# Eight batches written out in a cross-attention kernel, and a third of the query moves issued by ScalarE

## The chip, the cores and the metric

The kernel runs on one core of one Trainium2 chip. The metric is the device time of one execution in microseconds (us); lower is better. Before the change it is the median of three runs.

## The reference

Eight batches of 256 tokens of 256 features attend to 1601 context rows of 64 features, with 16 heads, and a small feed-forward network follows. Cut to what matters:

```python
q_big = jnp.einsum('bshk,hkq->bshq', (layernorm(x) @ Wq.T).reshape(b, s, H, K), w_kc_q)
kv_rope = kv_c * cos + rotate_half(kv_c) * sin
q_r = jnp.einsum('bshq,hqr->bhsr', q_big, W_qr)
k_r = jnp.einsum('bld,hdr->bhlr', kv_rope, W_kr)
attn = softmax(einsum('bhsr,bhlr->bhsl', q_r, k_r))
ctx_c = jnp.einsum('bhsl,bld->bhsd', attn, kv_rope)
x = x + einsum('bhsd,hkd->bshk', ctx_c, w_kc_kv).reshape(b, s, H * K) @ Wo.T
# ffn: thought = mlp(last token of layernorm(x)), 4 steps; gate = sigmoid(x @ gate_w + gate_b)
x = x + layer_norm(x + gate * (thought @ bc_w + bc_b))
```

## The kernel before

**The prologue** folds the weights, so that a head's query is one product of the normalised x with a 256x64 matrix, and the attended context is projected by one folded matrix. It then makes the queries of the first two head pairs.

**The main part** takes the 8 batches one after the other. A batch `n` has 8 head pairs (`p`, and `g = 8n + p` over all), a pair has 13 slots (`t`, the key tiles of 128 rows, the last of 65). In a slot TensorE (`pe`) does, in this order: the scores of tile `t` into one of two PSUM banks `ps_s` (lines 741 and 742, high and low parts of the queries in `qq[p % 4]`); a tile of scores of the *next* pair, only for its row maxima (`maxima`, line 614, into `ps_m`); and the products of probabilities and keys of the tile six slots back (`p_kv`, lines 660, 663 and 670). ScalarE (`act`) takes the exponential of each score tile (line 469); GpSimd, for two tiles of 13 VectorE, makes the low parts of the probabilities (line 210); VectorE reads the maxima (line 936). The scores of slot `t` may start when the exponential of slot `t - 2` is done, since that one frees the bank.

**The queries of pair g + 2** are made in slot 3 of pair g: six matmuls (line 602) into `ps_x`, a copy to `q_hi` by ScalarE (`high_part`, after the exponential of slot 3), and in slot 4 the rest to `q_lo` by VectorE (`low_part`). Both hold the two heads of a pair in rows 0 to 63 and 64 to 127. `qq` wants each head's 64 rows side by side in columns, the high part in rows 0 to 63 and once more in rows 64 to 127, the low part in rows 0 to 63. That is six DMAs of 64 rows by 512 bytes for a pair, all issued by SyncE (`sp`) in `move_queries` (lines 247 to 258): four for `q_hi` as soon as it is there, two for `q_lo`. They count on `in_qq[p % 2]`. TensorE waits for all six (line 748, in slot 10 of pair g) ahead of the first maxima of pair g + 2; ScalarE and VectorE wait for them much later, before they overwrite `q_hi` and `q_lo`.

**The loop.** Every engine's program goes through `batches` (line 212): batch 0 is written out, batches 1 to 6 are a hardware loop (`Fori`) of three rounds of two batches each, and batch 7 is written out. So a jump back is taken twice, between batches 2 and 3 and between batches 4 and 5. Waits in the loop compare with values computed from the loop's register.

**Other work in a batch**: in pair 4, after `high_part` of slot 3, ScalarE also normalises the rows of the batch before (`normalise_u`, line 510); in pair 6 it does a gate there, in pair 2 a copy in slot 2. SyncE loads the keys of the next batch (lines 237 and 238), and copies turned keys (`move_keys`).

**The end** is the last token's network, a chain of small steps, the gating, a layer norm and the store.

Of the kernel before, what the change touches and what calls it, by code (L numbers as in the profile page):

```python
# [15 lines left out]
B, S, DM = 8, 256, 256  # L16
# [6 lines left out]
NP = H // 2  # L23
# [31 lines left out]
def build_xattn_ffn(nc, x, kv, kv_last, cos_n, sin_n, ident_in, sel_in, wq, wkcq_t, wkckv, wqr, wkr_t, wo_t,  # L55
                    in_gamma, in_beta, agg_w, agg_b, pn_gamma, pn_beta, d1_w, d1_b, d2_w, d2_b,
                    bc_w, bc_b, gate_w, gate_b, out_gamma, out_beta, out):
    with ExitStack() as ctx:
# [150 lines left out]
            r = 128 if t < KT - 1 else LAST  # L209
            eng.tensor_tensor(probs_lo(t)[0:r, :], probs(t)[0:r, :], probs_hi(t)[0:r, :], ALU.subtract).then_inc(done, 1)  # L210

        def batches(eng, batch):

            batch(0, 0)
            with eng.Fori(0, (B - 2) // 2) as i:
                batch(i * 2 + 1, 1)
                batch(i * 2 + 2, 0)
            batch(B - 1, 1)

        def first(n):  # L220
            return isinstance(n, int) and n == 0

        def last(n):
            return isinstance(n, int) and n == B - 1


        @block.sync
        def _(sp):
            sp.dma_start(ident[:, :], ident_in).then_inc(in_small, 16)
            sp.dma_start(wkcq2[0:DCQ - 128], wkcq_t[128:DCQ]).then_inc(in_wa, 16)  # L230
            sp.dma_start(wqr2[0:DCQ - 128], wqr[128:DCQ]).then_inc(in_wa, 16)
            xv = xs[:, :].rearrange("p (b s m) -> p b s m", b=B, s=ST)
            for b in range(0, B, 2):
                sp.dma_start(xv[:, b:b + 2], x[b:b + 2].rearrange("b (s p) m -> p b s m", p=128)).then_inc(in_x[b // 2], 16)

            def load_keys(n):
                sp.dma_start(raw[:, 0:KT - 1, :], kv[n]).then_inc(in_raw, 16)
                sp.dma_start(raw[0:LAST, KT - 1, :], kv_last[n]).then_inc(in_raw, 16)

            sp.dma_start(sinn[:, :, :].rearrange("p t d -> p (t d)"), sin_n).then_inc(in_tab, 16)  # L240
            sp.dma_start(cosn[:, :, :].rearrange("p t d -> p (t d)"), cos_n).then_inc(in_tab, 16)
            sp.wait_ge(pads, 1)
            load_keys(0)
            sp.dma_start(wos, wo_t).then_inc(in_wc, 16)
            sp.dma_start(wkckvs, wkckv).then_inc(in_wc, 16)

            def move_queries(p, g):

                sp.wait_ge(qh_done, g + 1)
                if not (isinstance(g, int) and g < 4):  # L250
                    sp.wait_ge(st_done, g * KT - 3 * KT)
                d, r = qq[p % 4], p % 2
                for h in range(2):
                    for j in range(2):
                        sp.dma_start(d[64 * j:64 * j + 64, 0, h * S:(h + 1) * S], q_hi[r][64 * h:64 * h + 64, :]).then_inc(in_qq[r], 16)  # L255
                sp.wait_ge(ql_done, g + 1)
                for h in range(2):
                    sp.dma_start(d[0:64, 1, h * S:(h + 1) * S], q_lo[r][64 * h:64 * h + 64, :]).then_inc(in_qq[r], 16)

            def move_keys(n, par, i):  # L260

                sp.wait_ge(kt_copied, n * 2 + (i + 1))
                sp.dma_start(k_hx[par][0:64, key_half(i)], k_hl[par][0:64, key_half(i)]).then_inc(in_kx, 16)

            move_queries(0, 0)
            move_queries(1, 1)
            for i in range(2):
                move_keys(0, 0, i)
            sp.dma_start(gw[:, :, :], gate_w.rearrange("(t p) m -> p t m", p=128)).then_inc(in_gate, 16)
            sp.dma_start(gb[:, :], gate_b.partition_broadcast(128)).then_inc(in_gate, 16)  # L270
            for dst, src in ((aggs, agg_w), (bcs, bc_w)):
                sp.dma_start(dst[:, :, :], src.rearrange("(t p) m -> p t m", p=128)).then_inc(in_ffn, 16)
            for dst, src in ((ogs, out_gamma), (obs, out_beta)):
                sp.dma_start(dst[:, :], src.partition_broadcast(128)).then_inc(in_ffn, 16)
            for dst, src in ((ig8, in_gamma), (ib8, in_beta), (pg8, pn_gamma), (pb8, pn_beta), (ab8, agg_b), (db8, d2_b), (bb8, bc_b)):
                sp.dma_start(dst[:, :], src.partition_broadcast(B)).then_inc(in_ffn, 16)
            sp.dma_start(d1bs[:, :], d1_b).then_inc(in_ffn, 16)
            sp.dma_start(sels[:, :, :], sel_in).then_inc(in_ffn, 16)

            def batch(n, par):  # L280
                sp.wait_ge(prep, (n + 1) * PREP_OPS)
                if not last(n):
                    load_keys(n + 1)
                else:
                    for i, (src, w) in enumerate(((d1_w, HID), (d2_w, DM))):
                        sp.dma_start(tables[:, i * 2 * HID:(i + 1) * 2 * HID].rearrange("p (t m) -> p t m", m=w),
                                     src.rearrange("(t p) m -> p t m", p=128)).then_inc(in_dw, 16)
                for p in range(NP - 2 if last(n) else NP):
                    move_queries((p + 2) % NP, n * NP + p + 2)
                    if not last(n) and p in (3, 5):  # L290
                        move_keys(n + 1, 1 - par, (p - 3) // 2)

            batches(sp, batch)
            sp.wait_ge(x_saved, B)
            sp.dma_start(th[:, :], xs[127:128, :].rearrange("p (b s m) -> p b s m", b=B, s=ST)[:, :, ST - 1, :]).then_inc(in_row, 16)
            for b in range(B):
                sp.wait_ge(final[b % 2], b // 2 + 1)
                sp.dma_start(out[b].rearrange("(s p) m -> p s m", p=128),
                             gates[:, b * XB:(b + 1) * XB].rearrange("p (s m) -> p s m", s=ST)).then_inc(stored, 16)
            sp.wait_ge(stored, 16 * B)  # L300
# [3 lines left out]
        def _(pool):  # L304
# [45 lines left out]
                        if not first(n) and (p, t) in ROOT_SLOTS:  # L350
                            newton(n - 1, ROOT_SLOTS[p, t])

            batches(pool, batch)

            pool.wait_ge(pv_done, B * TB)
            for i in range(3):
# [25 lines left out]
        def _(act):  # L382
# [51 lines left out]
            def high_part(p, g):  # L434

                act.wait_ge(q_done, g + 1)
                copy(q_hi[p % 2][:, :], ps_x[:, 0:S], scale=SC / SW).then_inc(qh_done, 1)

            def copy_row(p, g):

                act.wait_ge(mrow_done, g + 1)
                copy(qq[p % 4][64:65, 1, :], ps_x[64:65, :], scale=1.0 / SC).then_inc(mrow_copied, 1)
# [4 lines left out]

            act.wait_ge(pads, 15)
            high_part(0, 0)
            high_part(1, 1)  # L450
            for i in range(2):
                copy_keys(0, 0, i, first_key_bank(i))
            for i in range(4):
# [5 lines left out]
            def batch(n, par):  # L459
                for p in range(NP):  # L460
                    g = n * NP + p
                    started = not (first(n) and p == 0)
                    for t in range(KT):
# [8 lines left out]
                        if t == 3 and not (last(n) and p >= NP - 2):  # L472
                            act.wait_ge(in_qq[p % 2], n * (QQ_DMAS * 4) + QQ_DMAS * (p // 2 + 1))
                            high_part(p, g + 2)
                        if t == 8 and started:
                            ctx_high(par if p else 1 - par, (p - 1) % NP, g - 1)
                        if t == 11 and not (last(n) and p == NP - 1):
# [21 lines left out]

            def save_x(m):  # L500
                act.wait_ge(post, m * POST_OPS + 1)
                copy(xs[:, bass.ds(m * XB, XB)], u[:, :, :].rearrange("p s m -> p (s m)")).then_inc(x_saved, 1)

            def normalise_u(m):
                act.wait_ge(root, m * ROOT_OPS + ROOT_OPS)
                for all_, one in ((rs_all, rs), (nm_all, nmu)):
                    copy(all_[:, bass.ds(m * ST, ST)], one[:, :]).then_inc(kept, 1)
                act.wait_ge(x_saved, m + 1)
                for st in range(ST):
                    act.activation(u[:, st, :], u[:, st, :], ACT.Identity, bias=nmu[:, st:st + 1],  # L510
# [2 lines left out]
            def gate(m):  # L513

                act.wait_ge(post, m * POST_OPS + 9)
                act.activation(gates[:, bass.ds(m * XB, XB)], z[:, :, :].rearrange("p s m -> p (s m)"),
                               ACT.Tanh, scale=0.5).then_inc(gate_out, 1)

            batches(act, batch)
            ctx_high(1, NP - 1, B * NP - 1)  # L520
            save_x(B - 1)
            for k in range(2 + K_STEPS):
# [23 lines left out]
        def _(pe):  # L546
# [52 lines left out]
            def queries(n, p, g):  # L599

                for i, (mt, wi, xi) in enumerate(SPLIT_MT):
                    mm = pe.matmul(ps_x[:, 0:S], mw[wi][:, mt, p * 128:(p + 1) * 128], xn_hl[xi][:, bass.ds(n * S + mt * B * S, S)],  # L602
                                   start=(i == 0), stop=(i == len(SPLIT_MT) - 1))
                mm.then_inc(q_done, 1)

            def maxima(par, p, g, j):

                if not (isinstance(g, int) and g == 0 and j < 3):

                    pe.wait_ge(mx_read, g * MX_OPS + {0: -3, 1: 0, 2: -1, MX_OPS - 1: MX_OPS - 2}.get(j, j - 2))  # L610
                if j < MX_OPS - 1:
# [179 lines left out]
                        else:  # L791
                            p_kv(n, par, p, t - LAG)

            batches(pe, batch)
            g = B * NP - 1
            for t in range(KT - LAG, KT):
                p_kv(B - 1, 1, NP - 1, t)
# [57 lines left out]
        def _(dve):  # L855
# [82 lines left out]
            def negate_max(p, g):  # L938

                dve.wait_ge(mx_read, g * MX_OPS + MX_OPS)  # L940
                if not (isinstance(g, int) and g == 0):
                    dve.wait_ge(mrow_done, g)
                with nc.allow_low_precision("a shift that cancels in the softmax"):
                    dve.tensor_reduce(negm[:, :], mxs[p % 2][:, :].rearrange("p (k i) -> p i k", k=4), AX.X, ALU.max,
# [6 lines left out]
            def normalise(p, g):  # L951
# [1 line left out]
                d = sums(p % 2)  # L953
                dve.wait_ge(pv_done, g * KT + KT)
                dve.reciprocal(inv[:, :, :], d[:, :, :, ONE]).then_inc(inv_done, 1)
                if not (isinstance(g, int) and g == 0):
                    dve.wait_ge(ct_done, g)
                dve.wait_ge(inv_done, g + 1)
                dve.tensor_tensor(ctx_m[:, :, :, :].rearrange("p s h d -> p h s d"), d[:, :, :, HIGH:OW],
# [7 lines left out]
            def post_a(m, psum):  # L967

                o = m * POST_OPS
                c = bass.ds(m * XB, XB)  # L970
                dve.wait_ge(proj_done, m * ST + ST)
                dve.wait_ge(st_done, m * TB + TB)
                dve.scalar_tensor_tensor(u[:, :, :], psum, 1.0 / SW, xs[:, c].rearrange("p (s m) -> p s m", s=ST), ALU.mult,
# [70 lines left out]
                            if p == 6 and t == 0:  # L1044
                                post_c(n - 1, ps_x[:, :])

            batches(dve, batch)
            g = B * NP - 1
            normalise(NP - 1, g)
            ctx_low(1, NP - 1, g)  # L1050
# [177 lines left out]
```

## Time and profile before

| | |
|---|---|
| median of 3 runs | 1167.55 us (1167.28 to 1168.71) |
| profiled execution, its own time | 1167.4 us |
| its span, first to last instruction | 1165.6 us |
| TensorE busy | 1073.1 us, 92% of the span |
| GpSimd, VectorE, ScalarE busy | 890.4, 886.5, 657.9 us |
| mean granted TensorE clock | 0.957 of 2.4 GHz |

The span and the time differ by 1.8 us around the program. The rows below come from one profiled execution. Busy shares tell which engine is full on the average; which wait sets the end is read from the waits and from the order in time. A transfer's issue is an instruction of the queue that issues it (SPq for SyncE, ACTq for ScalarE); its landing comes later.

### The profile page before, as it was taken

How to read it: one execution, taken by the hardware profiler on the slowest of the kernel's cores; microseconds unless marked ns; L12 is line 12 of the kernel's file. 1: busy time of each engine (PE TensorE's matmuls, PEld its weight loads, DVE VectorE, ACT ScalarE, POOL GpSimd, SP SyncE). 2: the span in 40 equal slices, each digit the busy share in tenths (PEclk: the TensorE clock that was granted, in tenths of full speed). 3: DMA queues.
4: the chain of work that ended last, by engine and by line, in shares of the span. 5: the costliest groups of instructions: out<-in, count | busy, mean ns of one | idle time of the engine just before them, and what ended most of it. 6: DMA issues, size and time to landing. Idle time of an engine off the chain costs nothing.

```text
span 1165.6 us, 39347 instructions
## 1 busy us (share of the span) xinstructions
PE 1073.1 (92%) x14644; PEld 714.8 (61%) x14644; DVE 886.5 (76%) x1573; ACT 657.9 (56%) x1179; POOL 890.4 (76%) x956
## 2 busy tenths in 40 slices
PE   5799999999999997999999989999999999999361
PEld 4446666666666665666666655666666667667240
DVE  5488888788868885788868776778878786887448
ACT  1546666566656664566656654566656665666322
POOL 0349988798889975898879876898879886878713
PEclk9989999999999998999999998999999999999655
DMA  9120001000100010000100010000100020000002
GB/s 340 48 78 15 21 18 30 16 21 15 30 12 21 18 31 12 14 21 19 30 11 21 17 33 16 9 21 19 30 16 21 15 89 11 15 16 2 1 2 72
DMA packets 42567, 36.37 MB, mean 31 GB/s; under 512 B 7864, under 2 KB 39416, under 8 KB 41920
## 3 DMA queue, kind: packets, MB, share of 16 engines
q1 hardware_dynamic: 41792, 29.49, 8.6%
q10 hardware_dynamic: 576, 4.19, 1.0%
q8 instruction: 129, 2.11, 0.8%
q14 instruction: 70, 0.57, 0.2%
HBM read 17.27 MB, written 2.10 MB: 17 GB/s over the span
## 4 chain that ended last, share of the span: by engine, by line
PE 81%; DVE 8%; issue 4%; DMA 4%; SPq 2%; ACT 1%; POOL 1%; DVEq 0%; ACTq 0%; POOLq 0%
PE ps_s L742 14%; PE ps_s L741 14%; PE ps_m L614 13%; PE ps_o L660 8%; PE ps_o L663 8%; PE ps_o L670 8%; PE ps_x L602 3%; PE ps_x L686 3%; DMA qq<-q_lo 2%; DVE mx L936 2%; PE ps_x L625 2%; SPq L255 1%; PE ps_x L678 1%; PE ps_x L713 1%; DMA plo_all<-wqr_dram 1%
## 5 line engine op out<-in xcount | busy, mean ns | idle before, releaser
L210 POOL TENSOR_TENSOR plo_all<-big 128x512 f16<-128x512 f32 x640 | 689.5, 1096 | 187.7 <-ACT big L469 186.7
L936 DVE TENSOR_REDUCE mx<-ps_m 128x1 f32<-128x512 f32 (+1 forms) x832 | 544.0, 666 | 199.8 <-PE ps_m L614 167.5
L469 ACT ACTIVATE big<-ps_s 128x512 f32<-128x512 f32 x768 | 458.0, 597 | 357.8 <-PE ps_s L742 356.8
L741 PE MATMUL ps_s<-qq,k_hl 128*128 128x512 f16 (+1 forms) x832 | 317.3, 381 | 12.6 <-issue 12.6
L742 PE MATMUL ps_s<-qq,k_hx 96*128 96x512 f16 (+1 forms) x832 | 319.0, 383 | 0.0
L614 PE MATMUL ps_m<-k_hl,qq 128*128 128x512 f16 x768 | 293.8, 383 | 6.7 <-DMA qq<-q_lo 5.5
L660 PEld LDWEIGHTS ps_o<-k,big 128*128 128x128 bf16 x3072 | 186.4, 98 | 122.4 <-issue 2.8
L663 PE MATMUL ps_o<-k,big 128*128 128x64 f16 x3072 | 220.0, 193 | 0.0
L670 PE MATMUL ps_o<-k,plo_all 128*128 128x65 f16 x3072 | 218.8, 193 | 0.0
L660 PE MATMUL ps_o<-k,big 128*128 128x65 f16 x3072 | 218.1, 193 | 0.0
L210 DVE TENSOR_TENSOR plo_all<-big 128x512 f16<-128x512 f32 x128 | 172.4, 1347 | 0.0
L663 PEld LDWEIGHTS ps_o<-k,big 128*128 128x128 bf16 x3072 | 146.6, 98 | 0.0
L670 PEld LDWEIGHTS ps_o<-k,plo_all 128*128 128x128 f16 x3072 | 145.0, 97 | 0.1
L614 PEld LDWEIGHTS ps_m<-k_hl,qq 128*128 128x128 f16 x768 | 76.4, 100 | 107.6 <-DVE mx L936 13.9
L741 PEld LDWEIGHTS ps_s<-qq,k_hl 128*128 128x128 f16 (+1 forms) x832 | 81.7, 98 | 14.4 <-issue 13.8
L742 PEld LDWEIGHTS ps_s<-qq,k_hx 96*128 96x128 f16 (+1 forms) x832 | 82.6, 99 | 1.0 <-issue 0.8
L323 POOL TENSOR_TENSOR tables<-tables 128x256 f32<-128x256 f32 (+3 forms) x64 | 55.1, 861 | 27.1 <-DMA tables<-kv_last_dram 26.5
L210 POOL TENSOR_TENSOR plo_last<-pr_last 65x512 f16<-65x512 f32 x64 | 66.4, 1037 | 1.4 <-ACT pr_last L469 1.3
L602 PE MATMUL ps_x<-xnt,mw 128*128 (+1 forms) x384 | 52.3, 272 | 2.4 <-DVE mw L915 1.4
L602 PEld LDWEIGHTS ps_x<-xnt,mw 128*128 128x128 f16 x384 | 37.1, 97 | 20.9 <-DVE mw L915 1.6
L469 ACT ACTIVATE pr_last<-ps_s 65x512 f32<-65x512 f32 x64 | 38.0, 593 | 14.0 <-PE ps_s L742 14.0
L390 ACT ACTIVATE qq<-ps_x 1x512 f16<-1x512 f32 x64 | 37.6, 588 | 5.7 <-PE ps_x L625 4.1
(189 smaller groups left out, 914.8 us busy)
## 6 DMA issues: line engine op xcount, KB each, us to landing
qq<-q_hi SPq DMA_DIRECT2D x256, 32.0 KB, 1.9
qq<-q_lo SPq DMA_DIRECT2D x128, 32.0 KB, 1.9
tables<-kv_dram SPq DMA_DIRECT2D x8, 384.0 KB
big<-wq_dram ACTq DMA_DIRECT2D x1, 2048.0 KB, 14.9
xs<-x_dram SPq DMA_DIRECT2D x4, 512.0 KB, 17.5
big<-wo_t_dram SPq DMA_DIRECT2D x1, 2048.0 KB, 12.9
tables<-d_w_dram SPq DMA_DIRECT2D x2, 1024.0 KB, 6.8
out_dram<-big SPq DMA_DIRECT2D x8, 256.0 KB, 2.2
```

The source lines that it names most:

```text
L210: eng.tensor_tensor(probs_lo(t)[0:r, :], probs(t)[0:r, :], probs_hi(t)[0:r, :], ALU.subtract).then_inc(done, 1)
L323: pool.tensor_tensor(*ops[k % 6]).then_inc(prep, 1)
L390: return act.activation(out_, in_, ACT.Copy, **kw)
L469: act.activation(probs(t)[0:r, :], ps_s[0:r, (p * KT + t) % 2, :], ACT.Exp, scale=1.0 / SC).then_inc(p_done, 1)
L602: mm = pe.matmul(ps_x[:, 0:S], mw[wi][:, mt, p * 128:(p + 1) * 128], xn_hl[xi][:, bass.ds(n * S + mt * B * S, S)], start=(i == 0), stop=(i ...
L614: mm = pe.matmul(ps_m[:, j % 3, :], qq[p % 4][:, 0, a:a + 128], k_hl[par][:, c:c + 512], start=True, stop=True)
L660: pe.matmul(d[:, q // 2, q % 2, :], probs_hi(t)[:, q * 128:(q + 1) * 128], k3[par][:, t, 0:OW], start=(t == 0 and q == 0), stop=False, ski ...
L663: pe.matmul(d[:, q // 2, q % 2, HIGH:OW], probs_hi(t)[:, q * 128:(q + 1) * 128], k3[par][:, t, LOW:LOW + DC], start=False, stop=False, ski ...
L670: mm = pe.matmul(d[:, q // 2, q % 2, :], probs_lo(t)[:, q * 128:(q + 1) * 128], k3[par][:, t, 0:OW], start=False, stop=(t == KT - 1), skip ...
L741: pe.matmul(ps_s[0:r, j % 2, :], k_hl[par][:, c], qq[p % 4][:, 0, :], start=True, stop=False)
L742: pe.matmul(ps_s[0:r, j % 2, :], k_hx[par][:, c], qq[p % 4][0:96, 1, :], start=False, stop=True).then_inc(st_done, 1)
L936: dve.tensor_reduce(o, i, AX.X, ALU.max).then_inc(mx_read, 1)
```

## The change

The loop is gone: `batches` calls each engine's program for `n` from 0 to 7, all waits and addresses are constants. The second of the two copies of the queries' high half (the one into rows 64 to 127 of `qq`) is issued by ScalarE: after `high_part` in the prologue, and in the main part in slot 4, after the exponential of that slot. SyncE issues the other four.

```diff
-        def batches(eng, batch):
-            batch(0, 0)
-            with eng.Fori(0, (B - 2) // 2) as i:
-                batch(i * 2 + 1, 1)
-                batch(i * 2 + 2, 0)
-            batch(B - 1, 1)
+        def batches(batch):
+            for n in range(B):
+                batch(n, n % 2)
...
                 for h in range(2):
-                    for j in range(2):
-                        sp.dma_start(d[64 * j:64 * j + 64, 0, h * S:(h + 1) * S], q_hi[r][64 * h:64 * h + 64, :]).then_inc(in_qq[r], 16)
+                    sp.dma_start(d[0:64, 0, h * S:(h + 1) * S], q_hi[r][64 * h:64 * h + 64, :]).then_inc(in_qq[r], 16)
                 sp.wait_ge(ql_done, g + 1)
...
+            def move_high(p, g):
+                act.wait_ge(qh_done, g + 1)
+                for h in range(2):
+                    act.dma_start(qq[p % 4][64:128, 0, h * S:(h + 1) * S], q_hi[p % 2][64 * h:64 * h + 64, :]).then_inc(in_qq[p % 2], 16)
...
             high_part(0, 0)
+            move_high(0, 0)
             high_part(1, 1)
+            move_high(1, 1)
...
                         if t == 3 and not (last(n) and p >= NP - 2):
                             act.wait_ge(in_qq[p % 2], n * (QQ_DMAS * 4) + QQ_DMAS * (p // 2 + 1))
                             high_part(p, g + 2)
+                        if t == 4 and not (last(n) and p >= NP - 2):
+                            move_high((p + 2) % NP, g + 2)
```

The rest of the diff replaces `isinstance` tests and `bass.ds` slices by plain ones, since every `n` is now a number.

## Rows read from the trace of the kernel before

**Rows 1.** The page, part 1: busy us, share of the span, instructions of each engine.
```profile
PE 1073.1 (92%) x14644; PEld 714.8 (61%) x14644; DVE 886.5 (76%) x1573; ACT 657.9 (56%) x1179; POOL 890.4 (76%) x956
```

**Rows 2.** TensorE's waits from 60 to 1060 us: total us, times, longest.
```profile
PE ps_s L741 <- issue: 12.6, 2, 6.7
...
PE ps_m L614 <- DMA qq<-q_lo: 1.6, 4, 0.6
```

**Rows 3.** Windows, one batch long each: us, busy us of each engine, then clock.
```profile
216.44:340.81 124.37, 123.95 (x1755) 83.16 (x1754) 100.06 (x171) 76.29 (x138) 107.30 (x115) 1.00 0.08 20
340.81:474.02 133.21, 126.27 (x1755) 84.27 (x1754) 99.43 (x171) 76.29 (x138) 106.94 (x115) 0.97 0.07 20
474.02:598.68 124.66, 124.03 (x1755) 83.15 (x1754) 100.05 (x171) 76.29 (x138) 107.39 (x115) 1.00 0.08 20
598.68:733.01 134.33, 126.67 (x1755) 84.34 (x1754) 99.33 (x170) 76.28 (x138) 106.62 (x115) 0.97 0.07 19
733.01:857.59 124.58, 124.03 (x1756) 83.16 (x1754) 100.14 (x171) 76.30 (x138) 107.42 (x115) 1.00 0.08 20
857.59:981.88 124.29, 123.90 (x1755) 83.12 (x1754) 99.22 (x170) 76.20 (x138) 104.59 (x112) 1.00 0.12 34
```

**Rows 4.** Timeline, first matmuls of batches 3 and 5: start, us; in brackets idle before.
```profile
442.57 0.61 PE L741 MATMUL ps_s<-qq,k_hl 128*128 128x512 f16 x1 [5.93 <-issue]
...
701.19 0.60 PE L741 MATMUL ps_s<-qq,k_hl 128*128 128x512 f16 x1 [6.67 <-issue]
```

**Rows 5.** Windows, right after the first of those: clock behind the busy times.
```profile
442.50:447.10 4.60, 4.53 (x32) 2.49 (x33) 1.38 (x2) 1.20 (x2) 1.80 (x2) 0.52 0.01 4
```

**Rows 6.** Timeline and line view: query moves by SyncE, durations in ns min/median/max.
```profile
514.33 2.38 SPq L255 DMA_DIRECT2D qq<-q_hi  x4
516.75 1.24 SPq L258 DMA_DIRECT2D qq<-q_lo  x2
...
L255 SPq DMA_DIRECT2D qq<-q_hi x256: 461/597/1767, 52.5 to 1038.3; - x128
```

**Rows 7.** Timeline, program start: issues of both queues.
```profile
0.75 0.41 SPq L229 DMA_DIRECT2D ident<-ident_in_dram  x1
0.75 0.41 ACTq L384 DMA_DIRECT2D big<-wkcq_t_dram  x1
...
1.85 0.91 SPq L231 DMA_DIRECT2D plo_all<-wqr_dram  x1
```

**Rows 8.** Timeline, ScalarE in slots 3 to 5 of pair 4, then slot 4 of pair 5.
```profile
514.31 1.08 ACT L510 ACTIVATE u<-u,nmu,rs 128x256 f32<-128x256 f32 x2
515.29 1.06 ACT L469 ACTIVATE big<-ps_s 128x512 f32<-128x512 f32 x2
...
529.47 0.60 ACT L469 ACTIVATE big<-ps_s 128x512 f32<-128x512 f32 x1 [0.41 <-PE ps_s L742]
```

**Rows 9.** Timeline, TensorE: scores of slots 4 and 7 of pair 4, slot 4 of pair 5.
```profile
514.00 0.38 PE L741 MATMUL ps_s<-qq,k_hl 128*128 128x512 f16 x1
...
517.05 0.38 PE L741 MATMUL ps_s<-qq,k_hl 128*128 128x512 f16 x1
...
528.84 0.38 PE L741 MATMUL ps_s<-qq,k_hl 128*128 128x512 f16 x1
```

**Rows 10.** Timeline, the prologue's query moves and what follows.
```profile
52.54 2.43 SPq L255 DMA_DIRECT2D qq<-q_hi  x4
...
53.90 0.38 ACT L390 ACTIVATE q_hi<-ps_x 128x256 f16<-128x256 f32 x1 [1.38 <-PE ps_x L602]
54.18 1.02 ACT L390 ACTIVATE k_hl<-ps_o 128x1024 f16<-128x1024 f16 x1
...
55.01 1.23 SPq L258 DMA_DIRECT2D qq<-q_lo  x2
55.08 0.71 ACT L390 ACTIVATE k_hl<-ps_m 128x640 f16<-128x640 f16 x1
...
57.77 0.59 PE L614 MATMUL ps_m<-k_hl,qq 128*128 128x512 f16 x1 [3.91 <-DMA qq<-q_lo]
```

More of the change, by code:

```diff
@@ L210, in make_low @@
             eng.tensor_tensor(probs_lo(t)[0:r, :], probs(t)[0:r, :], probs_hi(t)[0:r, :], ALU.subtract).then_inc(done, 1)
-        def batches(eng, batch):
-            batch(0, 0)
-            with eng.Fori(0, (B - 2) // 2) as i:
-                batch(i * 2 + 1, 1)
-                batch(i * 2 + 2, 0)
-            batch(B - 1, 1)
+        def batches(batch):
+            for n in range(B):
+                batch(n, n % 2)
         def first(n):
-            return isinstance(n, int) and n == 0
+            return n == 0
         def last(n):
-            return isinstance(n, int) and n == B - 1
+            return n == B - 1
         @block.sync
@@ L249, in move_queries @@
                 sp.wait_ge(qh_done, g + 1)
-                if not (isinstance(g, int) and g < 4):
+                if not (g < 4):
                     sp.wait_ge(st_done, g * KT - 3 * KT)
@@ L291, in batch @@
                         move_keys(n + 1, 1 - par, (p - 3) // 2)
-            batches(sp, batch)
+            batches(batch)
             sp.wait_ge(x_saved, B)
@@ L351, in batch @@
                             newton(n - 1, ROOT_SLOTS[p, t])
-            batches(pool, batch)
+            batches(batch)
             pool.wait_ge(pv_done, B * TB)
@@ L501, in save_x @@
                 act.wait_ge(post, m * POST_OPS + 1)
-                copy(xs[:, bass.ds(m * XB, XB)], u[:, :, :].rearrange("p s m -> p (s m)")).then_inc(x_saved, 1)
+                copy(xs[:, slice(m * XB, (m + 1) * XB)], u[:, :, :].rearrange("p s m -> p (s m)")).then_inc(x_saved, 1)
             def normalise_u(m):
@@ L506, in normalise_u @@
                 for all_, one in ((rs_all, rs), (nm_all, nmu)):
-                    copy(all_[:, bass.ds(m * ST, ST)], one[:, :]).then_inc(kept, 1)
+                    copy(all_[:, slice(m * ST, (m + 1) * ST)], one[:, :]).then_inc(kept, 1)
                 act.wait_ge(x_saved, m + 1)
@@ L515, in gate @@
                 act.wait_ge(post, m * POST_OPS + 9)
-                act.activation(gates[:, bass.ds(m * XB, XB)], z[:, :, :].rearrange("p s m -> p (s m)"),
+                act.activation(gates[:, slice(m * XB, (m + 1) * XB)], z[:, :, :].rearrange("p s m -> p (s m)"),
                                ACT.Tanh, scale=0.5).then_inc(gate_out, 1)
-            batches(act, batch)
+            batches(batch)
             ctx_high(1, NP - 1, B * NP - 1)
@@ L601, in queries @@
                 for i, (mt, wi, xi) in enumerate(SPLIT_MT):
-                    mm = pe.matmul(ps_x[:, 0:S], mw[wi][:, mt, p * 128:(p + 1) * 128], xn_hl[xi][:, bass.ds(n * S + mt * B * S, S)],
+                    mm = pe.matmul(ps_x[:, 0:S], mw[wi][:, mt, p * 128:(p + 1) * 128], xn_hl[xi][:, slice(n * S + mt * B * S, n * S + mt * B * S + S)],
                                    start=(i == 0), stop=(i == len(SPLIT_MT) - 1))
@@ L606, in maxima @@
             def maxima(par, p, g, j):
-                if not (isinstance(g, int) and g == 0 and j < 3):
+                if not (g == 0 and j < 3):
                     pe.wait_ge(mx_read, g * MX_OPS + {0: -3, 1: 0, 2: -1, MX_OPS - 1: MX_OPS - 2}.get(j, j - 2))
@@ L792, in batch @@
                             p_kv(n, par, p, t - LAG)
-            batches(pe, batch)
+            batches(batch)
             g = B * NP - 1
@@ L940, in negate_max @@
                 dve.wait_ge(mx_read, g * MX_OPS + MX_OPS)
-                if not (isinstance(g, int) and g == 0):
+                if not (g == 0):
                     dve.wait_ge(mrow_done, g)
@@ L955, in normalise @@
                 dve.reciprocal(inv[:, :, :], d[:, :, :, ONE]).then_inc(inv_done, 1)
-                if not (isinstance(g, int) and g == 0):
+                if not (g == 0):
                     dve.wait_ge(ct_done, g)
@@ L969, in post_a @@
                 o = m * POST_OPS
-                c = bass.ds(m * XB, XB)
+                c = slice(m * XB, (m + 1) * XB)
                 dve.wait_ge(proj_done, m * ST + ST)
@@ L1045, in batch @@
                                 post_c(n - 1, ps_x[:, :])
-            batches(dve, batch)
+            batches(batch)
             g = B * NP - 1
```

## The prediction

> **What bounds the kernel now.** I read the busy line of the page first: TensorE is busy for 92% of the span, the next engines for 76% [rows 1]. An average can hide a chain through other engines, so the second view is TensorE's waits in the main part. They are short, and two entries matter: 12.6 us in two pieces that wait for nothing the profile shows, and 1.6 us in four pieces for query moves [rows 2]. So over a thousand microseconds TensorE sets the pace, and ScalarE, VectorE and GpSimd count only where they make it wait. The third view cuts the main part into windows that start at the same matmul of each batch. Four of the six last 124.29 to 124.66 us, two last 133.21 and 134.33, with a lower clock in those two and nearly the same work [rows 3]. The timeline shows where: TensorE stands still for 5.93 and 6.67 us ahead of the first matmul of batches 3 and 5 [rows 4]. Those are the two places where a jump back to the loop's head is taken; at the boundaries 1 to 2, 3 to 4, 5 to 6 and 6 to 7, which the four short windows cross, there is no such gap. The last of these is the way out of the loop, so leaving it costs nothing that can be seen.
>
> **The loop written out.** The cost of a jump back is read as a whole from the windows, since it is more than the gap. After the gap TensorE runs at a granted clock of 0.52, that is at 1.2 GHz in place of 2.4, for some 4.6 us, after having been idle [rows 4, 5]. The mean of the four windows without a jump is (124.37 + 124.66 + 124.58 + 124.29) / 4 = 124.48 us. The two with one have 133.21 + 134.33 - 2 x 124.48 = 18.6 us more. Of that 12.6 is the gap, the other 6.0 is the slow clock and two waits for queries that come just behind it. With no jump I take off all 18.6. The low bound of this gain is 12.6, if the clock fell for some other reason; I see no room for more, since the other batches run without gaps. Batch 7 is already written out and takes the same time as a batch in the loop [rows 3]. That prices two things at nothing: constants instead of register values in the waits, and longer straight programs.
>
> **Two issues fewer on SyncE.** The four issues of the high part take 2.38 us, the two of the low part 1.24 [rows 6]; with two of the four gone the last one starts up to 1.2 us sooner. In the main part TensorE waits 1.6 us in all for these moves [rows 2]. Two of the four waits, 0.6 us each, stand in the two long windows and are in the 18.6 already. That leaves 0.4 us; the low part must still be made by VectorE first, so I take 0.2, with 0 and 0.4 as ends. SyncE itself is waiting nearly all the time, and nothing else queues behind these moves that TensorE is waiting for.
>
> In the prologue TensorE waits 3.91 us for the first pair's moves, until 57.77 [rows 10]. Now SyncE issues two high moves from 52.54 to 53.64 and two low ones to about 54.9, where it was 56.2; by that alone TensorE could start 1.3 us sooner. But ScalarE gets four issues in its path. The first two, from 52.5 to 53.6, end before its copy at 53.90. The next two come behind that copy, from about 54.3 to 55.4, and push the two key copies, which ran from 54.18 to 55.79, to 55.4 to 57.0. TensorE waits for both key copies too, so it starts at about 57.15. Gain 0.6, ends 0 and 1.3. The key copies are late next; they are what then ends the wait.
>
> **Two issues more on ScalarE in slot 4.** This is the unknown, 62 times. No row shows ScalarE issuing in the main part. The nearest are SyncE's moves of the same shape: 461 ns for the first of a group, 597 for one behind another [rows 6], so 0.46 + 0.04 + 0.60 = 1.10 us for two. What is queued behind them is the exponential of slot 5, and the scores of slot 7 wait for that one's bank; the low parts that GpSimd makes from it are needed six slots later and have time.
>
> In a usual pair the exponential of slot 4 starts at 529.47, 0.63 us behind its scores at 528.84; the scores of slot 7 start 3.05 us behind those of slot 4 (514.00 and 517.05) [rows 8, 9], so 2.42 us behind the exponential. Two ways to count. If the issues begin when the exponential has been handed over, the next exponential starts about 1.15 us behind it and not 1.02, ends at 1.75, and TensorE has 0.67 us left: cost nothing. If they begin only when it has ended, the next one starts at 0.60 + 0.04 + 1.10 + 0.04 = 1.78 and ends at 2.38. That leaves 0.04 us, from which the hand-over and a weight load, some 0.15 us, are to be paid: a stall of about 0.1 us.
>
> Pair 4 has less cover, because two normalisations of 1.08 us stand between, and the exponential of slot 4 starts at 515.29 [rows 8]. In the first way the next one ends at 515.29 + 1.15 + 0.10 + 0.60 = 517.14, while TensorE wants it at 517.05 [rows 9]: a stall of 0.2 us with the hand-over. In the second it ends at 517.67: 0.75 us. This happens in seven batches.
>
> So the cost is 7 x 0.2 = 1.4 us in the first way, and 55 x 0.1 + 7 x 0.75 = 10.8 in the second. The low end is 0, if the issues can start ahead of the exponential. I take 1.4: in the trace ScalarE's next activation starts before the one before has ended (two in 1.06 us, at 0.60 each [rows 8]), so its queue runs ahead of the engine. A few issues are longer, up to 1767 ns [rows 6]; ScalarE has a third of the issues, and what one of these costs beyond the 0.67 us of cover is some 0.5 us. That is for the range.
>
> **The sum**: 1167.4 - 18.6 - 0.2 - 0.6 + 1.4 = 1149.4 us against the profiled execution's own time (span 1165.6 and 1.8 around it). The median of the runs is 0.15 above that one, so 1149.6.
>
> **Rivals.** *The issues take ScalarE's own time* (the second way): 1149.6 - 1.4 + 10.8 = 1159.0 us. For it: nothing rules out that the queue waits for the engine. Against it: the overlapping activations.
>
> *The two queues exclude each other at issue*, the one that ends slower. Place: slot 4, where SyncE's first high move starts at about 529.17, 0.30 ahead of the exponential. Taken in turns, SyncE from -0.30 to 0.16, ScalarE to 0.8, SyncE to 1.4, ScalarE to 2.05, the exponential of slot 5 ends at 2.75, against 2.42 wanted: with the hand-over a stall of 0.48 us. Times 55, and 0.35 for the seven pairs 4, where SyncE is nearly done first: 29 us, so 1149.6 - 1.4 + 29 = 1177 us. It decides from 0.3 us for each pair on, where it eats the 18 us. Against it: at the program's start both queues have an issue from 0.75 to 1.16, 0.41 us each, side by side; for a little of it: SyncE's third took 0.91 [rows 7].
>
> The Trainium skill, page Perfetto Trace Analysis, section DMA Instruction — HWDGE (DVE, Sync), says that the block that generates descriptors is shared by two sequencers and locked for exclusive use while it is used; that is this rival, and only part of an issue's time would be under the lock. The trace agrees at most in the 0.91 us.
>
> *The gap is not the jump's*, and stays: 1167.6 - 0.8 + 1.4 = 1168 us. Against it: four boundaries of the same code have no gap. *The longer program stalls elsewhere*, by half of what is won: 1158 us; against it, batches 0 and 7 are straight code without such gaps.
>
> **How the numbers follow.** The forecast with its ends (issues between 0 and 4 us) has 0.74, and 1146.5 to 1152.5 us. The issues in ScalarE's own time: 0.14, near 1159. Exclusion of the queues: 0.05 for its full price, and 0.02 for one that just cancels the gain. A gap that stays: 0.01. Stalls elsewhere: 0.04. The range of 8 in 10 is 1146.5 to 1158. 0.2% of this time is 2.3 us, about what can be told from no change; faster by more gets 0.92, within it 0.03, slower 0.05.
>
> **What would show it.** Right: no window of a batch above 125 us; no wait "issue" of microseconds on TensorE; clock near 1.00 from 75 to 1060 us; in slot 4 the exponential of slot 5 starting about 1.15 us behind that of slot 4. Wrong: waits of TensorE's line 741 for ScalarE, some 60 of them; ScalarE's issues at 1 us each; windows of 126 us or more with no gap in them. In the prologue the wait for `qq` should turn into one for `k_hl`, until about 57.15.

## The result and the profile after

The changed kernel takes 1148.38 us (median of 4 runs, 1147.16 to 1152.49), the kernel before beside it 1167.41 us (4 runs). The ratio is 0.9847 with a 95% interval of 0.9816 to 0.9877: 1.5% faster, against a forecast of 1149.6 us. The profiled execution took 1147.16 us with a span of 1145.4. On another chip the same kernel (e8 below) took 1150.49 us, with a ratio of 0.9863 (0.9847 to 0.988): a gain of 16.0 us there and of 19.0 us here. The profiled execution is the fastest of all eight.

The page of the kernel after, part 1, as in [rows 1]:

```profile
PE 1067.0 (93%) x14644; PEld 713.7 (62%) x14644; DVE 883.4 (77%) x1573; ACT 656.4 (57%) x1179; POOL 889.1 (78%) x956
```

TensorE's waits from 60 to 1045 us, which answer to [rows 2]:

```profile
PE ps_x L684 <- DVE ctx_m L965: 1.4, 6, 0.2
PE ps_s L747 <- ACT big L473: 1.4, 3, 0.6
```

The 12.6 us that waited for nothing are gone, and so are the waits for query moves. A small new one stands in their place: three waits for ScalarE's exponential, 1.4 us.

The windows of one batch each, from the same matmul as in [rows 3]:

```profile
215.75:339.91 124.16, 123.93 (x1756) 83.31 (x1754) 98.90 (x170) 76.08 (x138) 107.00 (x115) 1.00 0.08 20
339.91:464.09 124.18, 123.89 (x1755) 83.28 (x1754) 99.82 (x170) 76.09 (x138) 106.45 (x114) 1.00 0.08 20
464.09:588.89 124.80, 124.02 (x1755) 83.28 (x1754) 99.41 (x170) 76.08 (x138) 107.47 (x116) 1.00 0.08 20
588.89:713.05 124.16, 123.55 (x1756) 83.64 (x1754) 100.07 (x170) 75.77 (x138) 106.75 (x115) 1.00 0.08 20
...
sum 745.77, PE 743.25 PEld 500.06 DVE 596.82 ACT 456.34 POOL 639.34; mean PE 123.87 PEld 83.34 DVE 99.47 ACT 76.06 POOL 106.56
```

The second and fourth windows, which held the jumps and took 133.21 and 134.33 us, now take 124.18 and 124.16 at a clock of 1.00. All six sum to 745.77 us, where those of [rows 3] sum to 765.44. That is 19.7 of the 20.2 us between the two profiled executions.

ScalarE in a usual pair (timeline, exponentials of slots 4 and 5) and in pair 4, where the two normalisations stand in the way [rows 8]:

```profile
489.85 0.60 ACT L473 ACTIVATE big<-ps_s 128x512 f32<-128x512 f32 x1 [0.35 <-PE ps_s L748]
489.86 1.12 ACTq L439 DMA_DIRECT2D qq<-q_hi  x2
491.08 0.60 ACT L473 ACTIVATE big<-ps_s 128x512 f32<-128x512 f32 x1 [0.63 <-PE ps_s L748]
...
504.71 0.47 ACTq L439 DMA_DIRECT2D qq<-q_hi  x1
504.92 0.59 ACT L516 ACTIVATE u<-u,nmu,rs 128x256 f32<-128x256 f32 x1
505.21 0.61 ACTq L439 DMA_DIRECT2D qq<-q_hi  x1
505.42 1.11 ACT L473 ACTIVATE big<-ps_s 128x512 f32<-128x512 f32 x2
```

The two issues start 0.01 us after the exponential of slot 4 has started, and the next exponential comes 1.23 us behind it. In pair 4 they start before that exponential does, while a normalisation runs. In the usual pair SyncE's two high moves run beside ScalarE's, 0.33 us ahead of them, and neither pair of issues is drawn out:

```profile
489.53 1.10 SPq L251 DMA_DIRECT2D qq<-q_hi  x2
```

The prologue, as in [rows 10]:

```profile
52.34 1.15 SPq L251 DMA_DIRECT2D qq<-q_hi  x2
52.34 1.41 ACTq L439 DMA_DIRECT2D qq<-q_hi  x2
...
54.22 1.13 ACTq L439 DMA_DIRECT2D qq<-q_hi  x2
54.80 1.47 SPq L251 DMA_DIRECT2D qq<-q_hi  x2
...
55.39 1.02 ACT L386 ACTIVATE k_hl<-ps_o 128x1024 f16<-128x1024 f16 x1 [1.21 <-issue]
56.31 0.70 ACT L386 ACTIVATE k_hl<-ps_m 128x640 f16<-128x640 f16 x1
...
57.11 0.39 PE L620 MATMUL ps_m<-k_hl,qq 128*128 128x512 f16 x1 [3.45 <-ACT k_hl L386]
```

The wait is for the key copies now, as forecast, and ends at 57.11 us, where 57.77 stood. Of these 0.66 us, 0.20 are not the change's: the first query matmuls already start at 51.00 us in this execution and at 51.20 in the one before, so the change gives 0.46.

Here the two queues do get in each other's way, a little. Single issues behind another take 0.60 us on SyncE in the kernel before, and 0.62 in ScalarE's pair from 54.22. But ScalarE's second issue, which starts at 52.91, 0.02 us behind SyncE's second one, takes 0.84 us, and SyncE's from 54.80, 0.07 us behind one of ScalarE's, takes 0.83. That makes the 1.41 and the 1.47 above. No code is fetched in this stretch, and the 1.41 or 1.42 us stand in the same place in e2, e6, e8, e9, e10 and e12.

### The profile page after: what moved, and what is told of

Same layout as the page of the kernel before. It is cut to its first block, busy times and chain, and to the rows that moved or that the text cites. A ratio compares the mean times of both kernels' runs of the same rounds, so it can differ in the third digit from the quotient of the medians.

```text
span 1145.4 us, 35018 instructions
## 1 busy us (share of the span) xinstructions
PE 1067.0 (93%) x14644; PEld 713.7 (62%) x14644; DVE 883.4 (77%) x1573; ACT 656.4 (57%) x1179; POOL 889.1 (78%) x956
## 4 chain that ended last, share of the span: by engine, by line
PE 86%; DVE 8%; issue 2%; ACT 2%; DMA 1%; POOL 1%; ACTq 1%; SPq 0%; DVEq 0%; POOLq 0%
PE ps_s L748 15%; PE ps_s L747 15%; PE ps_m L620 14%; PE ps_o L666 9%; PE ps_o L669 8%; PE ps_o L676 8%; PE ps_x L608 3%; PE ps_x L692 3%; DVE mx L942 2%; PE ps_x L631 2%; PE ps_x L684 1%; PE ps_x L719 1%; DMA plo_all<-wqr_dram 1%; PE ps_s L564 1%; PE ps_s L565 1%
## 5 line engine op out<-in xcount | busy, mean ns | idle before, releaser
L210 DVE TENSOR_TENSOR plo_all<-big 128x512 f16<-128x512 f32 x128 | 168.1, 1314 | 0.0
L608 PE MATMUL ps_x<-xnt,mw 128*128 128x256 f16 x384 | 52.2, 272 | 2.4 <-DVE mw L921 1.4
```

## The experiments

Each is compared with the kernel before on its own chip; its median there was 1167.69, 1166.48 and 1167.17 us for the three sets (e1 to e4, e5 to e8, e9 to e12).

### e1, e2: each half of the change alone

e1 takes the kernel before and writes the loop out on all engines; the moves stay with SyncE. e2 keeps the loop and has only the issues moved.

```diff
# e1
-            batch(0, 0)
-            with eng.Fori(0, (B - 2) // 2) as i:
...
-            batch(B - 1, 1)
+            for n in range(B):
+                batch(n, n % 2)
...
# e2
...
+                        if t == 4 and not (last(n) and p >= NP - 2):
+                            move_high((p + 2) % NP, g + 2)
```

> All engines written out, all six moves issued by SyncE as before. Theory (the jumps are the cost, the issues are hidden): nearly the whole gain, 18 to 19 us, so 1148.5 to 1149.5 us; the wait for queries in the prologue stays, TensorE starts the first maxima at about 57.7 us. Rival (the issues on ScalarE give a good part of the gain): 1155 us or more.

> The loop as before, ScalarE issues the two second copies. Theory: 0.7 us less from the prologue and about as much lost or won in the main part, so within 1.5 us of the kernel before, 1166 to 1168 us, with two gaps of 5.9 and 6.7 us. Rival (the issues give a good part of the gain): 1160 us or less.

e1: 1150.56 us (1149.95 to 1150.63), ratio 0.9848 (0.9831 to 0.9864), 17.1 us less than the kernel before. The loop written out gives the whole gain, within what can be told: the changed kernel gained 19.0 us on one chip and 16.0 on another. Its six windows span 745.77 us (963.63 - 217.86), the same as those of the changed kernel.

e2: 1175.92 us (1168.03 to 1178.49, six runs), ratio 1.0068 (1.0047 to 1.0088). This is a miss of my theory: I expected no change within 1.5 us. The issues alone make the loop kernel 8 us slower in the median, and their cost differs much from run to run. With e9 and e10, which are the same kernel, the median of eight runs is 1173.98 us. The profile is that of the fastest run, and has 8 waits for ScalarE, 3.1 us. e9 and e10 go on from here.

### e3, e4: whose jump it is

In e3 TensorE's program alone is written out, in e4 all others are.

```diff
-        def batches(eng, batch):
+        def batches(eng, batch, flat=False):
+            if flat:
+                for n in range(B):
+                    batch(n, n % 2)
+                return
...
# e3: only this call, e4: the four others
-            batches(pe, batch)
+            batches(pe, batch, True)
```

> TensorE's program alone is written out, the other four engines keep their loop; moves as before. Theory (the gap is TensorE's own, at its jump; what the others lose is hidden by their slack or comes out as a small wait): at most 1151 us, gap gone. Rival (another engine's jump costs as much and only hides beside TensorE's): the gap stays as a wait for ScalarE, VectorE or GpSimd, 1160 us or more.

> Only TensorE keeps the loop, the other four engines are written out; moves as before. Theory: as the kernel before, 1166 to 1168.5 us, with both gaps. Rival (other engines' jumps count): some part of the 18.6 us is gone, 1160 us or less.

e3: 1151.46 us (1150.81 to 1151.78), ratio 0.9855 (0.9838 to 0.9871). e4: 1166.03 us (10 runs), ratio 0.9985 (0.9975 to 0.9995). So TensorE's own jumps carry nearly everything: writing out its program alone gives 16.2 us, writing out the four others alone 1.7. The two windows with the jump in e3, then in e4; the one between them, without a jump, takes 124.16 us in e3 and 124.23 in e4:

```profile
342.02:467.46 125.44, 124.06 (x1756) 83.32 (x1754) 99.22 (x171) 76.02 (x138) 107.24 (x115) 1.00 0.08 20
591.62:716.84 125.22, 124.12 (x1756) 83.26 (x1754) 99.50 (x171) 76.12 (x138) 107.24 (x115) 1.00 0.08 20
```

```profile
342.16:475.09 132.93, 126.39 (x1755) 84.25 (x1754) 99.55 (x171) 76.15 (x138) 106.83 (x115) 0.97 0.07 19
599.32:731.20 131.88, 125.89 (x1755) 84.09 (x1754) 99.98 (x171) 76.15 (x138) 107.14 (x115) 0.97 0.08 19
```

With TensorE running straight, a jump of the others shows as 1.1 to 1.3 us in a window. It is a wait for ScalarE, here around the first of them, in e3:

```profile
PE ps_s L745 <- ACT big L473: 1.0, 1, 1.0
```

What TensorE does in the gap can be seen in part in the DMA view, which lists packets that carry instructions (queue, packets, MB, share). First the gap of the kernel before, 436.4 to 442.6 us, then that of e4, 437 to 444:

```profile
q14 instruction: 7, 0.06, 3.5%
q8 instruction: 2, 0.03, 2.5%
```

```profile
q8 instruction: 2, 0.03, 2.1%
```

In e4, where only TensorE jumps, queue 14 is silent and queue 8 still brings two packets; in e3, where the others jump, queue 14 brings its seven (436 to 442 us). So queue 8 carries TensorE's code, and two blocks of it are fetched while TensorE stands still. The two fetches do not fill the gap of 5.9 us; what the rest of it is stays open.

### e7: one jump in place of two

The loop has two rounds; batches 5 to 7 are written out behind it.

```diff
-            with eng.Fori(0, (B - 2) // 2) as i:
+            with eng.Fori(0, 2) as i:
                 batch(i * 2 + 1, 1)
                 batch(i * 2 + 2, 0)
-            batch(B - 1, 1)
+            for n in range(5, B):
+                batch(n, n % 2)
```

> The kernel before with a loop of two rounds (batches 1 to 4) and batches 5 to 7 written out: one jump back, between batches 2 and 3. Theory (each jump costs 9 us, the loop's code nothing): 9 to 10 us less than before, about 1157.5 us, one gap. Rival (the second gap comes from the place in time, not from the jump): both gaps stay, no change.

1157.68 us (1156.66 to 1159.03), 8.8 us less than the kernel before beside it, where 9 to 10 were expected; ratio 0.9928 (0.9911 to 0.9945). The window between batches 2 and 3 still takes 133.17 us, the one between 4 and 5 takes 124.28:

```profile
341.40:474.57 133.17, 125.93 (x1755) 84.03 (x1754) 100.16 (x171) 76.28 (x138) 106.99 (x115) 0.97 0.07 20
598.94:723.22 124.28, 123.92 (x1755) 83.13 (x1754) 99.99 (x171) 76.38 (x138) 107.31 (x115) 1.00 0.08 20
```

The gap follows the jump, not the place in time; a loop that is entered, and left behind its last round, costs nothing that can be seen.

### e5, e11: what the issues would cost with no cover left

e5 is the changed kernel with all four high moves issued by ScalarE in slot 4.

```diff
-                for h in range(2):
-                    sp.dma_start(d[0:64, 0, h * S:(h + 1) * S], ...)
+                if g < 2:
+                    for h in range(2):
+                        sp.dma_start(d[0:64, 0, h * S:(h + 1) * S], ...)
...
                 for h in range(2):
-                    act.dma_start(qq[p % 4][64:128, 0, h * S:(h + 1) * S], ...)
+                    for j in range(2 if g >= 2 else 1):
+                        r0 = 64 - 64 * j
+                        act.dma_start(qq[p % 4][r0:r0 + 64, 0, h * S:(h + 1) * S], ...)
```

> The changed kernel, but in the main part ScalarE issues all four high moves of a pair (some 2.4 us in place of 1.1), SyncE the two low ones. Theory (the issues start beside the exponential of slot 4, 0.67 us of cover are left): the exponential of slot 5 ends about 3.1 us behind the start of that of slot 4, wanted at 2.42, a stall of 0.7 to 0.8 us in each of 62 pairs: 1190 to 1200 us, with TensorE's line of the high scores waiting for ScalarE. Rival (ScalarE's queue runs further ahead, or an issue does not hold up the next activation): under 1160 us.

1230.32 us (1226.1 to 1234.01), ratio 1.0545 (1.0512 to 1.0578). The direction and the place were right, the size was not. ScalarE's timeline in a usual pair, and TensorE's waits from 75 to 1110 us:

```profile
504.85 0.60 ACT L476 ACTIVATE big<-ps_s 128x512 f32<-128x512 f32 x1 [0.35 <-PE ps_s L751]
504.86 2.41 ACTq L442 DMA_DIRECT2D qq<-q_hi  x4
507.37 1.09 ACT L476 ACTIVATE big<-ps_s 128x512 f32<-128x512 f32 x2 [1.92 <-PE ps_s L751]
```

```profile
PE ps_s L750 <- ACT big L476: 45.4, 61, 2.1
PE ps_m L623 <- DVE mx L945: 21.6, 6, 4.5
```

The first wait is the expected one, 45.4 / 61 = 0.74 us a pair: an issue does hold up the next activation, but not the one that runs. The second wait was expected by nobody. Its longest piece, on VectorE and GpSimd (timeline):

```profile
543.44 7.90 DVE L210 TENSOR_TENSOR plo_all<-big 128x512 f16<-128x512 f32 x1
551.26 1.87 DVE L945 TENSOR_REDUCE mx<-ps_m 128x1 f32<-128x512 f32 x3
```

```profile
544.21 0.86 POOL L320 TENSOR_TENSOR tables<-tables 128x320 f32<-128x320 f32 x1
545.03 2.05 POOL L210 TENSOR_TENSOR plo_all<-big 128x512 f16<-128x512 f32 x2
547.02 1.05 POOL L210 TENSOR_TENSOR plo_last<-pr_last 65x512 f16<-65x512 f32 x1
548.02 0.78 POOL L320 TENSOR_TENSOR k<-tables,k 128x320 f16<-128x320 f32 x1
548.74 2.05 POOL L210 TENSOR_TENSOR plo_all<-big 128x512 f16<-128x512 f32 x2
```

VectorE's low-part instruction (median 1.43 us) takes 7.90 us, to 551.34, while GpSimd has one instruction right behind the other until the last one shown ends at 550.79. A run of GpSimd without a pause is not enough by itself: in the profile of the changed kernel seven low parts of GpSimd follow one another from 146.45 us, and VectorE's, started at 147.88, is through in 2.15 us. e11 tests whether less work on GpSimd ends the long ones: the same kernel, with the low part of one more slot moved from GpSimd to VectorE.

```diff
-LO_D = (2, 9)
+LO_D = (2, 7, 9)
```

> The variant in which ScalarE issues all four high moves (1230 us), with one more low part of the probabilities (slot 7) moved from GpSimd to VectorE. If VectorE's low-part instructions of 8 us are waits for a GpSimd that works without a pause, giving GpSimd an eighth less to do there gives it pauses: these instructions fall to 3 us or less, the waits for the maxima go, and the time falls by 15 us or more, to 1215 us or less. Rival (they have another cause, or VectorE is full): 1225 us or more.

1198.16 us (1197.64 to 1200.2), ratio 1.0272 (1.0255 to 1.0289): 32 us less than e5, although VectorE has 64 instructions more. The low-part instructions of VectorE, min/median/max in ns, and TensorE's waits:

```profile
L210 DVE TENSOR_TENSOR plo_all<-big x192: 677/1353/2736, 78.2 to 1105.7; 128x512 f16<-128x512 f32 x192
```

```profile
PE ps_s L750 <- ACT big L476: 45.0, 62, 1.7
```

The wait for the exponential stays, 45.0 us in 62 pieces, and the waits for the maxima are gone. That bears out that the long instructions come from the work on GpSimd. Whether it is the pauses or the other order of the work that helps was not told apart.

### e6, e12: the prologue

e6 is the changed kernel with the key copies ahead of `move_high(1, 1)`. e12 has ScalarE issue only in the prologue; in the main part SyncE issues all six.

```diff
# e6
             high_part(1, 1)
-            move_high(1, 1)
             for i in range(2):
                 copy_keys(0, 0, i, first_key_bank(i))
+            move_high(1, 1)
# e12
-                        if t == 4 and not (last(n) and p >= NP - 2):
-                            move_high((p + 2) % NP, g + 2)
...
+                    for j in range(1 if g < 2 else 2):
+                        sp.dma_start(d[64 * j:64 * j + 64, 0, h * S:(h + 1) * S], ...)
```

> The changed kernel, but in the prologue ScalarE copies the keys ahead of the second pair's two issues. Theory (the key copies end TensorE's wait at 57.1 us): they end 1.1 us sooner and the wait goes back to the query moves, first maxima at about 56.4 us, 0.5 to 0.8 us less than the changed kernel, about 1147.7 us. Rival (something else ends that wait, or the time is given back before slot 0): no change.

> All engines written out, ScalarE issues only in the prologue, SyncE issues all six moves in the main part. Theory: the prologue's 0.5 us is kept and ScalarE's late activations are gone: 1149.5 to 1150.5 us, the same as the changed kernel within what can be measured, with no wait of TensorE for ScalarE in the main part.

e6: 1148.93 us (1146.42 to 1150.03), ratio 0.9845 (0.9829 to 0.9862); e8 beside it, the changed kernel once more, 1150.49. The wait turned back into one for the moves, 2.8 us where it had been 3.4, which is the 0.6 us expected. (The first maxima come at 57.86 us and not at the expected 56.4, since the query matmuls start at 52.35 us in this execution, 1.35 us later than in the profile of the changed kernel.) Whether the end comes sooner by as much can't be told at this spread.

e12: 1149.3 us (1148.57 to 1150.59), ratio 0.9845 (0.9829 to 0.9862), with no wait of TensorE for ScalarE in the main part. It is as fast as the changed kernel within what can be told. Its four runs lie within 2.0 us, those of the changed kernel within 5.3 and, in e8, within 2.9; four runs are too few to call that a difference in spread.

### e8: the changed kernel again

> The changed kernel once more, beside the other variants of this call: 1148.4 us, the reference for differences under one microsecond.

1150.49 us (1149.64 to 1152.52), ratio 0.9863 (0.9847 to 0.988). Its profiled execution is the slowest of the eight of this kernel, 1152.52 us, and shows what the fastest does not. TensorE's waits from 75 to 1060 us:

```profile
PE ps_x L558 <- DVE q_lo L931: 2.6, 2, 1.4
...
PE ps_s L747 <- ACT big L473: 0.3, 1, 0.3
```

The two waits for `q_lo` stand at 155.1 and 651.7 us, each behind a long low part on VectorE, 3.25 and 3.47 us, beside six instructions of GpSimd without a pause. Here is the second (VectorE, GpSimd):

```profile
647.28 3.47 DVE L210 TENSOR_TENSOR plo_all<-big 128x512 f16<-128x512 f32 x1
...
647.17 6.47 POOL L210 TENSOR_TENSOR plo_all<-big 128x512 f16<-128x512 f32 x6
```

This is the stall of e5, smaller, in the changed kernel itself. The first of the two, of 1.2 us in pair 5 of batch 0, stands in the profiles of e2, e6, e8, e9 and e10, in all of which ScalarE issues in the main part, and in none of the kernel before, e1, e3, e4, e7 and e12, in which it does not; only the fastest execution of the changed kernel goes without it. So it goes with ScalarE's issues; by what steps an activation that is 0.2 us late leads to it was not followed.

The two stalls are half of what parts this execution from the fastest. Of the 5.4 us between them, 4.35 arise ahead of batch 1 (its first matmul comes at 191.50 us here, at 187.15 there): the first matmul of all waits for a load until 13.62 and not 12.60 us, the granted clock is at 0.5 from 53.6 to 63.9 us and not from 57.3 to 60.7, and the stall of 1.2 us is there.

### e9, e10: why the issues cost so differently

Both are e2 once more, one run each.

> The loop as before with ScalarE's two issues, once more: that kernel ran from 1168.0 to 1178.5 us, and its profile was of the fastest run. Theory A (an issue that meets the fetch of a block of TensorE's code takes 1.5 to 2 us, and how many of ScalarE's issues meet one differs from run to run): a run above 1172 us shows more than 8 waits of TensorE for ScalarE, in all 6 us or more. Theory B (late activations make GpSimd run without a pause, and a low-part instruction on VectorE waits for it for many microseconds): such a run shows low-part instructions on VectorE of 5 us and more, and TensorE waiting for the maxima.

> The same kernel a third time, for a second look at its spread: as above.

e9 took 1169.38 us, e10 1174.31, so e10 is a run above 1172 us with a profile. It has 7 waits for ScalarE, 2.6 us; e9 has 5, 1.8 us. So theory A does not make the difference. Theory B does, in one place of e10: the window of 859.71 to 988.97 takes 129.26 us where the same window of the kernel before takes 124.29 [rows 3], and in it stand, on VectorE, on GpSimd and on TensorE (timeline):

```profile
914.33 5.52 DVE L210 TENSOR_TENSOR plo_all<-big 128x512 f16<-128x512 f32 x1
```

```profile
914.27 6.47 POOL L210 TENSOR_TENSOR plo_all<-big 128x512 f16<-128x512 f32 x6
...
920.91 0.28 PE L561 MATMUL ps_x<-identh,k 128*128 128x128 f16 x2 [3.53 <-DVE q_lo L934]
```

The longest such instruction is 5.5 us in e10, 3.3 in e9, 3.2 in e2's profiled run, 2.2 in the kernel before. One stall accounts for 5 us, which is the difference between e10 and e9. What a run of 1178 us holds was not seen in a profile; that it is two or three of these stalls is a guess. It also stays open why the loop kernel pays more for the two issues than the written-out one. It has somewhat more long pairs of issues on ScalarE, of 1.4 us and more: 11, 10 and 9 of 62 in e2, e9 and e10, against 7, 6 and 9 in the changed kernel, e8 and e6.

Of theory A one half holds. In the main part of the changed kernel's profile 20 of 185 pairs of issues take from 1.4 to 2.4 us, on either queue, and every one of them overlaps a packet of queue 8, the fetch of a block of TensorE's code. This is one of them (ScalarE's timeline, then the DMA view of 599.6 to 602.2: queue, packets, MB, share):

```profile
599.69 2.43 ACTq L439 DMA_DIRECT2D qq<-q_hi  x2
602.22 1.08 ACT L473 ACTIVATE big<-ps_s 128x512 f32<-128x512 f32 x2 [1.94 <-PE ps_s L748]
```

```profile
q8 instruction: 1, 0.02, 3.6%
```

Of the 165 shorter pairs, 20 overlap such a fetch as well. So a fetch goes with the long issues, and does not always make one.

## Why the prediction was right

**The jumps.** The step was 18.6 us in the windows. Shown: e1, with nothing else changed, has windows shorter by 765.44 - 745.77 = 19.7 us. The size was short by 1.1 us, because I took the jump-free windows of the loop (124.48) as what is left, and straight code runs at 124.3.

In whole times e1 gains less, 17.1 us by the medians and 17.5 between the profiled executions: its first window starts 1.4 us later than that of the kernel before (217.86 and 216.44), and 0.8 us more follow its last one. The part ahead of batch 1 differs by up to 4.35 us between two executions of one kernel (e8), so this is no sign against the windows; but it means that the step is known to a microsecond or two and no better, and that a sum which meets the median within 1.2 us on one chip, and misses it by 0.9 the other way on another, is in part lucky.

The attribution to the jump is shown by e7, and that it is TensorE's own by e3 and e4. That other engines' jumps hide was only assumed; e3 prices them at about 1.2 us a window once TensorE's is gone. The Trainium skill, page Runtime: NRT & Kernel Launch, section Instruction fetch mechanics, says that a taken branch out of the small window of fetched code waits for a fetch by DMA. The traces agree in what they show: 5.93 and 6.67 us [rows 4] at the jumps, two packets of TensorE's code in the first of these gaps, and no such gap in straight code.

One reading of mine was not what the rows say. I took the time of batch 7 from [rows 3], whose last window ends 28.6 us into it. Its scores, from first to last, take 121.25 us before and after the change, so the conclusion stands, that straight code there costs nothing. And half of what is won would have put stalls of the longer program at 1158.6 us, not 1158.

**The moves in the main part.** I took 0.2 us. With the loop gone e1 and e12 still wait 0.8 and 1.0 us for them, the changed kernel not at all, so the term was too small by 0.6 to 0.8 us.

**The prologue.** Forecast was a start at 57.15 us and 0.6 gained, with the key copies ending the wait. It ended at 57.11, by the key copies, with 0.46 us from the change and 0.20 from an execution that was ahead already.

**ScalarE's issues.** I took 1.4 us, from 7 stalls in pairs 4. The sum is met by chance: in the fastest execution the waits for ScalarE are 1.4 us, but in three places elsewhere, the two larger ones (0.5 and 0.6 us) behind long issues. In e8's they are 0.3 us, and 2.6 us of waits for `q_lo` come with them. In pair 4 ScalarE's queue is ahead of its engine and the issues cost nothing, which was the low bound. In a usual pair the first way of counting holds, 1.23 us from one exponential to the next where I had 1.15. The occasional long issue was in the range; that issues on ScalarE could end in a drawn-out instruction of VectorE was in no step. The changed kernel pays less for it than e2: its longest is 3.2 us and delays nothing, e8's two cost 2.6 us together, the one of e10 3.5.

**The rivals.** Issues in ScalarE's own time: refuted by the timeline, 0.01 us between the starts. Queues that exclude each other: refuted at the price that I gave, since in slot 4 the two pairs take 1.10 and 1.12 us side by side, 0.33 us apart. But there is something in it: in the prologue, where second issues start within 0.1 us of an issue of the other queue, they take 0.83 and 0.84 us and not 0.60. By the Trainium skill's rule of the exclusive lock, on the page Perfetto Trace Analysis, section DMA Instruction — HWDGE (DVE, Sync), one of two issues waits while the other uses the block; the trace agrees with such a wait of 0.2 us, and not of a whole issue. The gap that stays: refuted by the windows. Stalls of the longer program: refuted for batches 1 to 7; ahead of them the profiles differ too much from run to run to tell a microsecond.

**The two halves.** The forecast was the sum, and did not say that the second half is worth nothing in the main part. That is what e1 and e12 show: moving issues to ScalarE gives the prologue's half microsecond. In the main part it saves 0.8 to 1.0 us of waits for moves and costs 1.4 us in the one profile, 2.9 in the other. In the loop kernel (e2) it costs 6 to 8 us and brings a spread of 10; in the written-out one no such spread is shown.

## What to carry to other kernels

Where one engine is full and its program is a hardware loop, look for gaps ahead of the loop's first instruction: here a jump back cost 9 to 10 us, a third of it slow clock and waits behind the gap, and writing out the program of that engine alone gave nearly all of it back. Take the price from windows from one batch to the next, not from the gap. An issue on ScalarE's queue runs beside the running instruction and delays the next: here two of them nearly always fit into the slack, four cost 0.74 us each time. One profile of a kernel can miss a cost: the stalls of 2.6 us stand in e8's and not in the first one. Before delaying an engine, look at who runs close to full behind it; here that was GpSimd at 78%, and VectorE waits for it.

## What was not expected of the hardware

A two-input instruction of VectorE in SBUF, 0.68 us at its shortest and 1.43 in the median, took up to 7.90 us while GpSimd ran instructions without a pause, and ended 0.55 us behind the last of these. It does not wait for one GpSimd instruction only: eight ended meanwhile. In e10 it was five, and the sixth, the last of the 6.47 us, began at 919.26 and took 1.48 us, longer than the usual 1.04: there VectorE got in between. The Trainium skill, page SBUF — State Buffer, section Who interferes with whom, says that a VectorE instruction with two SBUF inputs contends with a GpSimd instruction that reads SBUF, and calls the port pair that they share an exclusive lock. The runs agree, and show that VectorE can lose several times in a row.

A pair of issues that takes 1.1 us in the median took up to 2.43 us in stretches in which a block of code was fetched, on SyncE and ScalarE alike.
